# Second buffers for the activated rows of layer 2 in a two-layer graph network on one core

## The chip, the core and the metric

The kernel runs on one core of a Trainium2 chip. The core has a matrix engine (PE, with its weight loads PEld), a vector engine (DVE), an activation engine (ACT), a general engine (POOL) and a sync engine (SP) that here only issues transfers; 16 DMA engines move the data. The metric is the device time of one execution in microseconds (us), as the median of several runs.

## The reference, cut to what matters

```python
h = relu(layernorm(x)); x = x + attention_layer(h, src, dst)          # layer 1
h = relu(layernorm(x))                                                # layer 2
hW = h @ W_kernel + W_bias                  # (50000, 256)
h_self, h_all = split(hW, 2)
msg = h_all[src] + (edge_attr @ We_kernel + We_bias)
deg = in_degree[dst]
x = x + h_self + segment_sum(msg * clip(deg, 1), dst)
```

There are 50,000 nodes of 128 features and 50,000 edges, sorted by `dst`. Only layer 2 is touched by the change.

## The kernel before, in words

The kernel has three stages in a row: a table of keys and values (up to about 600 us of the profile), layer 1 (to about 1190 us) and layer 2 (from about 1200 us to the end). Each engine has its own program, written out by hand, and the programs are held together by counters (semaphores): `wait(engine, counter, value)` holds an engine until a counter has reached a value, `.then_inc(counter, 1)` raises it when an instruction is done.

Layer 2 works in 50 batches of 10 tiles; a tile is 100 nodes and the window of 128 edges that end in them. For batch k and tile t:

- SP loads the 100 x 10 node rows with their two layernorm numbers into `xn1` (`nodes1`, L692 to L695, four slots; the load of batch m waits until batch m-4 has been summed), ten windows of edge features into `eaw` (`features`, L685 to L690, four slots) and stores the result (`store1`, L697 to L701).
- POOL gathers, for each tile, the 128 rows of the edges' source nodes by an indirect transfer into `xs1` (`gathers1`, L820 to L827, four slots). Before each second gather t of batch k it waits until ACT has used tiles up to t+1 of batch k-4.
- ACT makes two activated tiles (`relu1`, L1697 to L1709): `hn1` from the node rows (L1704) and `hs1` from the gathered rows (L1707). Before each even tile it waits on `R.ha`, the counter of PE's pairs (L1703).
- DVE builds the one-hot edge-to-node matrix `member` (L1384) and moves PE's results out of the banks: `rows_out` (L1394), `features_out` (L1402), `turned_out` (L1410) and `sums` (L1420), which adds the node rows and gives the output.
- PE works in steps (`step1`, L2025 to L2045). Step k starts with `features_sum(k, 0)` (L1987), then come five `rows_sum` (L1991 to L2001), each of two tiles: it transposes `hn1` (L1998) and multiplies `hs1` by `member` (L1999) into one bank and raises `R.ha` by one. Between them stand the projections `project1` (L2010 to L2012) of this batch and the one before, and `turn_back` (L2021).

`hn1` and `hs1` have room for one batch (`hn1 = hn`, `hs1 = vw`, L233 and L234), so ACT may write tile t of batch k only when PE has read tile t of batch k-1. That makes ACT at most one batch ahead of PE, and POOL, which trails ACT by four slots, at most five.

Of PE's matmuls, one step has 78: 20 at L1987, 10 at L1998, 20 at L1999, 18 at L2010 to L2012 and 10 at L2021. The order of the work is fixed for each engine; only the waits decide when it runs. Layer 2's PE program is a loop over four steps for batches 2 to 45 (L2102 to L2105); ACT's, DVE's and POOL's are written out in full.

Two more tiles in on-chip memory have no user in layer 2: the part of `q` behind `oT` (columns 1200 on) and `prod`, both last used in layer 1. ACT starts layer 2 only after `long_done[0]` (L1753), when layer 1 is over.

Of the kernel before, what the change touches and what calls it, by code (L numbers as in the profile page):

```python
# [11 lines left out]
ACT = mybir.ActivationFunctionType  # L12
AX_X = mybir.AxisListType.X

N, D, E, HEADS, DE = 50000, 128, 50000, 4, 64
CH = D // HEADS
NODES = 100
TILES = N // NODES
WIN = 128
B = 10  # L20
# [44 lines left out]
def wait(eng, sem, value):  # L65

    if not isinstance(value, int) or value > 0:
        eng.wait_ge(sem, value)
# [66 lines left out]
def build(nc, x, edges, ea, Wq, bq, Wk, bk, Wv, bv, Ws, bs, W1, b1, We, be, out):  # L135
# [7 lines left out]
    with ExitStack() as ctx:  # L143
        def sb(name, shape, dt=F32):
            return ctx.enter_context(nc.sbuf_tensor("sb_" + name, shape, dt))

        def bank(name):
            return ctx.enter_context(nc.psum_tensor("ps_" + name, [128, 512], F32))
# [5 lines left out]
        ident = sb("ident", [128, 128])  # L154
# [19 lines left out]
        q_raw = sb("q", [128, 2 * B * D])  # L174
# [14 lines left out]
        vw = vw_raw[:].rearrange("e (t c) -> e t c", t=B)  # L189
        prod = prod_raw[:].rearrange("e (t c) -> e t c", t=B)  # L190
        hn = hn_raw[0:NODES, :].rearrange("n (t c) -> n t c", t=B)
# [37 lines left out]
        xs1 = kv_raw[:, 0:4 * B * XW].rearrange("e (s t c) -> e s t c", s=4, t=B)  # L229
        eaw = kv_raw[:, 4 * B * XW:4 * B * (XW + EW)].rearrange("e (s t c) -> e s t c", s=4, t=B)  # L230
        xn1 = xn_raw[0:NODES, 0:4 * B * XW].rearrange("n (s t c) -> n s t c", s=4, t=B)
        y1 = xo_raw[0:NODES, 0:4 * B * D].rearrange("n (s t c) -> n s t c", s=4, t=B)
        hn1 = hn  # L233
        hs1 = vw  # L234
        haT = hT_raw[:, 0:3 * 8 * NODES].rearrange("c (g h t n) -> c g h t n", g=3, h=2, t=4)
        aeT = mT_raw[0:EW + 1, 0:2 * B * NODES].rearrange("c (s t n) -> c s t n", s=2, t=B)
        oT = q_raw[:, 0:3 * 4 * NODES].rearrange("c (g t n) -> c g t n", g=3, t=4)
# [99 lines left out]
        banks = [bank(f"b{n}") for n in range(8)]  # L337
# [120 lines left out]
        P, A, R = Table(), Attend(), Message()  # L458
# [1125 lines left out]
        def _(act):  # L1584
# [112 lines left out]
            def relu1(k, t):  # L1697
                if t == 0:
                    act.wait_ge(R.xn[k % 4], 16 * (k // 4 + 1))
                if t % 5 == 0:  # L1700
                    act.wait_ge(R.xs[k % 4][t // 5], 16 * 5 * (k // 4 + 1))
                if t % 2 == 0:
                    wait(act, R.ha, 5 * (k - 1) + t // 2 + 1)  # L1703
                nc.scalar.activation(hn1[:, t, :], xn1[:, k % 4, t, 0:D], ACT.Relu,  # L1704
                                     scale=xn1[:, k % 4, t, D:D + 1], bias=xn1[:, k % 4, t, D + 1:XW]
                                     ).then_inc(R.relu, 1)
                nc.scalar.activation(hs1[:, t, :], xs1[:, k % 4, t, 0:D], ACT.Relu,  # L1707
                                     scale=xs1[:, k % 4, t, D:D + 1], bias=xs1[:, k % 4, t, D + 1:XW]
                                     ).then_inc(R.relu, 1)  # L1709

# [43 lines left out]
            for k in range(BATCHES):  # L1754
                for t in range(B):
                    relu1(k, t)
# [4 lines left out]
        def _(pe):  # L1761
# [229 lines left out]
            def rows_sum(s, j):  # L1991
                k = s.k
                n = 5 * k + j
                pe.wait_ge(R.relu, s.count(2 * B, 4 * j + 4))
                wait(pe, R.ha_sb, s.count(5, j - 1))
                for t in (2 * j, 2 * j + 1):
                    at = (t % 2) * NODES
                    nc.tensor.transpose(banks[n % 2][:, at:at + NODES], hn1[:, t, :], ident[0:NODES, 0:NODES])  # L1998
                    ins = nc.tensor.matmul(banks[n % 2][:, at + 2 * NODES:at + 3 * NODES], hs1[:, t, :],  # L1999
                                           member[:, (k + 3) % 4, t, :], start=True, stop=True)  # L2000
                ins.then_inc(R.ha, 1)  # L2001

# [128 lines left out]
```

## Time and profile before

| | us |
|---|---|
| three runs without a profile | 2101.73, 2109.67, 2113.67 |
| their median | 2109.67 |
| the profiled execution, device time | 2092.29 |
| its span, first to last instruction | 2090.5 |
| layer 2 in it | about 890 |

The profiled execution is 17.4 us below the median and 9.4 us below the lowest of the three runs. Spans and starts in a profile are microseconds from its first instruction. A row of the timeline has the start, the duration, the engine, the line, what is written and read, the count of merged instructions and, in brackets, how long the engine had been idle and what released it. "issue" and "remote" as a releaser mean that the profile found no instruction that had just ended.

### The profile page before, as it was taken

How to read it: one execution, taken by the hardware profiler on the slowest of the kernel's cores; microseconds unless marked ns; L12 is line 12 of the kernel's file. 1: busy time of each engine (PE TensorE's matmuls, PEld its weight loads, DVE VectorE, ACT ScalarE, POOL GpSimd, SP SyncE). 2: the span in 40 equal slices, each digit the busy share in tenths (PEclk: the TensorE clock that was granted, in tenths of full speed). 3: DMA queues.
4: the chain of work that ended last, by engine and by line, in shares of the span. 5: the costliest groups of instructions: out<-in, count | busy, mean ns of one | idle time of the engine just before them, and what ended most of it. 6: DMA issues, size and time to landing. Idle time of an engine off the chain costs nothing.

```text
span 2090.5 us, 34477 instructions
## 1 busy us (share of the span) xinstructions
PE 1562.4 (75%) x10545; PEld 1324.3 (63%) x10546; DVE 1347.9 (64%) x3688; ACT 1031.2 (49%) x2501; POOL 1092.3 (52%) x1202
## 2 busy tenths in 40 slices
PE   6888883777787778877778514777877887777787
PEld 4677663667777777776777513666665665555665
DVE  8877631777777787777778703555555555555565
ACT  6787872444444444445444123544444454444453
POOL 2544425556665666655665075555555555555530
PEclk9999996999999999999999856998998888999999
DMA  8898872445455554545454142555554454555442
GB/s 240 276 300 274 299 227 80 130 130 149 135 147 144 145 146 139 150 133 148 130 151 127 56 107 67 121 124 134 121 119 118 120 124 118 130 123 121 119 113 62
DMA packets 162552, 302.85 MB, mean 145 GB/s; under 512 B 104113, under 2 KB 107703, under 8 KB 157524
## 3 DMA queue, kind: packets, MB, share of 16 engines
q1 hardware_dynamic: 121503, 201.19, 33.0%
q0 software_dynamic: 40896, 99.90, 19.7%
q8 instruction: 62, 1.02, 0.2%
q14 instruction: 91, 0.75, 0.1%
HBM read 196.84 MB, written 104.12 MB: 144 GB/s over the span
## 4 chain that ended last, share of the span: by engine, by line
PE 41%; DVE 20%; issue 18%; another core or an unknown queue 14%; DMA 4%; ACT 1%; SPq 1%; POOL 1%; DVEq 0%; ACTq 0%; POOLq 0%
PE ps_b L1891 6%; PE ps_b L1999 5%; PE ps_b L1987 4%; PE ps_b L2010 3%; PE ps_b L1791 3%; PE ps_b L2011 3%; PE ps_b L2012 3%; DMA sb_kv<-in_x 3%; PE ps_b L2021 3%; DVE sb_member L1175 2%; PE ps_b L1924 2%; PE ps_b L1998 2%; PE ps_b L1879 2%; DVE sb_q L1410 2%
## 5 line engine op out<-in xcount | busy, mean ns | idle before, releaser
L797 POOL DMA_INDIRECT sb_kv<-kv_rows,sb_src_all x500 | 502.4, 1005 | 363.6 <-DVE sb_vw L1235 146.3
L825 POOL DMA_INDIRECT sb_kv<-x_rows,sb_src_all x500 | 473.4, 947 | 403.6 <-ACT sb_vw L1707 201.4
L1704 ACT ACTIVATE sb_hn<-sb_xn 100x128 f32<-100x128 f32 x500 | 242.1, 484 | 485.6 <-remote 195.4
L1394 DVE COPY sb_hT<-ps_b 128x400 f32<-128x400 f32 x250 | 142.1, 569 | 196.2 <-remote 79.7
L1707 ACT ACTIVATE sb_vw<-sb_kv 128x128 f32<-128x128 f32 x500 | 239.4, 479 | 0.0
L1632 ACT ACTIVATE sb_hn<-sb_xn,sb_nstat 100x128 f32<-100x128 f32 x500 | 231.2, 494 | 0.0
L1791 PE MATMUL ps_b<-sb_w,sb_memberT 128*125 128x256 f32 x800 | 199.0, 387 | 22.0 <-DVE sb_xn L915 12.1
L2021 PE MATMUL ps_b<-sb_ident,sb_q 128*100 128x128 f32 x500 | 93.0, 306 | 141.6 <-DVE sb_q L1410 100.7
L1924 PE MATMUL ps_b<-sb_vw,sb_member 128*100 128x128 f32 x1000 | 140.2, 292 | 70.0 <-DVE sb_vw L1235 70.0
L1999 PE MATMUL ps_b<-sb_member,sb_vw 128*128 128x100 f32 x1000 | 185.7, 291 | 0.0
L1654 ACT COPY sb_memberT<-ps_b 100x512 f32<-100x512 f32 x150 | 76.1, 508 | 208.9 <-PE ps_b L1879 123.7
L1924 PEld LDWEIGHTS ps_b<-sb_vw,sb_member 128*100 128x100 f32 x1000 | 123.7, 179 | 79.9 <-DVE sb_vw L1235 79.9
L1791 PEld LDWEIGHTS ps_b<-sb_w,sb_memberT 128*125 128x125 f32 x800 | 144.7, 191 | 44.8 <-issue 18.3
L1999 PEld LDWEIGHTS ps_b<-sb_member,sb_vw 128*128 128x128 f32 x1000 | 166.4, 209 | 9.8 <-issue 9.8
L1998 PE MATMUL ps_b<-sb_ident,sb_hn 100*128 100x100 f32 x500 | 133.1, 266 | 49.7 <-issue 39.8
L1187 DVE TENSOR_TENSOR sb_prod<-ps_b,sb_kv 128x512 f32<-128x512 f32 x150 | 89.3, 596 | 118.8 <-PE ps_b L1891 65.3
L2021 PEld LDWEIGHTS ps_b<-sb_ident,sb_q 128*100 128x100 f32 x500 | 58.8, 141 | 159.6 <-DVE sb_q L1410 93.5
L1987 PE MATMUL ps_b<-sb_member,sb_kv 128*65 128x100 f32 x1000 | 119.9, 274 | 49.0 <-issue 18.3
L1987 PEld LDWEIGHTS ps_b<-sb_member,sb_kv 128*65 128x65 f32 x1000 | 108.4, 156 | 74.2 <-issue 54.7
L1384 DVE TENSOR_SCALAR sb_member<-sb_iota,sb_drel_all,sb_wdeg_all 128x100 f32<-128x100 f32 x500 | 145.0, 339 | 0.1
L1646 ACT COPY sb_q<-ps_b 100x512 f32<-100x512 f32 x150 | 76.2, 508 | 133.0 <-remote 100.8
L1235 DVE TENSOR_TENSOR sb_vw<-sb_kv,ps_b 128x1280 f32<-128x1280 f32 x50 | 74.4, 1488 | 101.9 <-remote 97.4
(184 smaller groups left out, 3428.8 us busy)
## 6 DMA issues: line engine op xcount, KB each, us to landing
kv_rows<-sb_kv SPq DMA_DIRECT2D x26, 1120.0 KB
sb_xn<-x_rows SPq DMA_DIRECT2D x50, 507.8 KB
sb_xn<-in_x SPq DMA_DIRECT2D x50, 500.0 KB
out_rows<-sb_xo SPq DMA_DIRECT2D x49, 500.0 KB
x_rows<-sb_xo SPq DMA_DIRECT2D x24, 1015.6 KB
sb_kv<-in_edge_attr SPq DMA_DIRECT2D x500, 32.0 KB
sb_kv<-in_x SPq DMA_DIRECT2D x28, 560.0 KB
kv_rows<-sb_xn SPq DMA_DIRECT2D x13, 1120.0 KB
```

Of the source, the lines that this page charges most:

```text
L797: pool.indirect_dma_start(out=kvs[:, k % 4, t, :], out_offset=None, in_=kv_rows, in_offset=bass.IndirectOffsetOnAxis(ap=src_all[:, n:n + 1 ...
L825: pool.indirect_dma_start(out=xs1[:, k % 4, t, :], out_offset=None, in_=x1, in_offset=bass.IndirectOffsetOnAxis(ap=src_all[:, n:n + 1], ax ...
L1384: ins = dve.tensor_scalar(member[:, (k + 3) % 4, t, :], iota[:], drel_all[:, n:n + 1], wdeg_all[:, n:n + 1], ALU.is_equal, ALU.mult)
L1632: nc.scalar.activation(hn[:, t, :], xn[:, k % 5, t, :], ACT.Relu, scale=nstat[:, n, 0:1], bias=nstat[:, n, 1:2]).then_inc(A.relu, 1)
L1704: nc.scalar.activation(hn1[:, t, :], xn1[:, k % 4, t, 0:D], ACT.Relu, scale=xn1[:, k % 4, t, D:D + 1], bias=xn1[:, k % 4, t, D + 1:XW]).th ...
L1707: nc.scalar.activation(hs1[:, t, :], xs1[:, k % 4, t, 0:D], ACT.Relu, scale=xs1[:, k % 4, t, D:D + 1], bias=xs1[:, k % 4, t, D + 1:XW]).th ...
L1791: ins = nc.tensor.matmul(banks[2 + n % 4][0:ROWS, (t % 2) * 2 * D:(t % 2 + 1) * 2 * D], hpT[:, (3 * b + g) % 4, (t - first) * ROWS:(t - fi ...
L1924: ins = nc.tensor.matmul(ps[0:NODES, (t - first) * D:(t - first + 1) * D], member[:, k % 3, t, :], vw[:, t, :], start=False, stop=t == las ...
L1987: ins = nc.tensor.matmul(banks[2 + n % 2][0:EW, (t - 5 * i) * NODES:(t - 5 * i + 1) * NODES], eaw[:, k % 4, t, :], member[:, (k + 3) % 4, ...
L1998: nc.tensor.transpose(banks[n % 2][:, at:at + NODES], hn1[:, t, :], ident[0:NODES, 0:NODES])
L1999: ins = nc.tensor.matmul(banks[n % 2][:, at + 2 * NODES:at + 3 * NODES], hs1[:, t, :], member[:, (k + 3) % 4, t, :], start=True, stop=True)
L2021: ins = nc.tensor.transpose(banks[6 + (3 * k + g) % 2][0:NODES, t * D:(t + 1) * D], oT[:, g, t, :], ident[:])
```

## The change

The rows of layer 2 that ACT makes get a second buffer each, used by odd batches. The second `hn1` is 1280 columns of `q` behind `oT`, the second `hs1` is `prod`. ACT's wait on `R.ha` looks back two batches where it looked back one, so for batches 0 and 1 it is gone. PE reads the buffer of its batch.

```diff
-        hn1 = hn
-        hs1 = vw
+        hn1 = (hn, q_raw[0:NODES, 3 * 4 * NODES:3 * 4 * NODES + B * D].rearrange("n (t c) -> n t c", t=B))
+        hs1 = (vw, prod)
...
                 if t % 2 == 0:
-                    wait(act, R.ha, 5 * (k - 1) + t // 2 + 1)
-                nc.scalar.activation(hn1[:, t, :], xn1[:, k % 4, t, 0:D], ACT.Relu,
+                    wait(act, R.ha, 5 * (k - 2) + t // 2 + 1)
+                nc.scalar.activation(hn1[k % 2][:, t, :], xn1[:, k % 4, t, 0:D], ACT.Relu,
...
-                nc.scalar.activation(hs1[:, t, :], xs1[:, k % 4, t, 0:D], ACT.Relu,
+                nc.scalar.activation(hs1[k % 2][:, t, :], xs1[:, k % 4, t, 0:D], ACT.Relu,
...
-                    nc.tensor.transpose(banks[n % 2][:, at:at + NODES], hn1[:, t, :], ident[0:NODES, 0:NODES])
-                    ins = nc.tensor.matmul(banks[n % 2][:, at + 2 * NODES:at + 3 * NODES], hs1[:, t, :],
+                    nc.tensor.transpose(banks[n % 2][:, at:at + NODES], hn1[k % 2][:, t, :], ident[0:NODES, 0:NODES])
+                    ins = nc.tensor.matmul(banks[n % 2][:, at + 2 * NODES:at + 3 * NODES], hs1[k % 2][:, t, :],
                                            member[:, (k + 3) % 4, t, :], start=True, stop=True)
```

## Rows read from the trace of the kernel before

**Rows 1.** The page: span, then busy tenths of PE and POOL in 40 slices

```profile
span 2090.5 us, 34477 instructions
...
PE   6888883777787778877778514777877887777787
...
POOL 2544425556665666655665075555555555555530
```

**Rows 2.** Windows of layer 2: columns PE, PEld, DVE, ACT, POOL busy, PEclk, DMA share, GB/s

```profile
1299.30:2015.02 715.72, 557.23 (x3354) 443.11 (x3355) 399.20 (x989) 348.35 (x861) 406.88 (x430) 0.90 0.51 122
2029.69:2064.97 35.28, 33.70 (x235) 27.51 (x234) 27.73 (x69) 24.42 (x60) 0.00 (x0) 1.00 0.30 84
```

**Rows 3.** Waits from 1300 to 2000 us: total, times, longest

```profile
POOL sb_kv L825 <- ACT sb_vw L1707: 183.6, 78, 4.5
ACT sb_hn L1704 <- remote: 166.4, 42, 7.3
ACT sb_hn L1704 <- PE ps_b L1999: 158.3, 81, 4.9
```

**Rows 4.** PE's first use of ACT's rows, L1998, from 1300 to 2000 us

```profile
L1998 PE MATMUL ps_b<-sb_ident,sb_hn x422: 248/252/375, 1300.2 to 1997.9; 100*128 100x100 f32 x141
its engine sat idle before it (us, times) until:
  issue: 0.3, 2
  DVE sb_hT L1394: 0.2, 1
```

**Rows 5.** Timeline of one step in the middle of layer 2, 1503 to 1521 us

```profile
1503.51 0.94 POOL L825 DMA_INDIRECT sb_kv<-x_rows,sb_src_all  x1 [3.12 <-ACT sb_vw L1707]
...
1505.27 0.32 SPq L695 DMA_DIRECT2D sb_xn<-x_rows  x1
...
1509.01 0.64 PE L2021 MATMUL ps_b<-sb_ident,sb_q 128*100 128x128 f32 x4 [1.19 <-issue]
...
1515.37 0.94 POOL L825 DMA_INDIRECT sb_kv<-x_rows,sb_src_all  x1 [0.30 <-issue]
...
1517.87 0.69 DVE L1420 TENSOR_TENSOR sb_xo<-ps_b,sb_xn 100x512 f32<-100x512 f32 x1 [4.59 <-remote]
...
1518.22 0.49 ACT L1704 ACTIVATE sb_hn<-sb_xn 100x128 f32<-100x128 f32 x1 [4.37 <-remote]
...
1520.13 0.97 POOL L825 DMA_INDIRECT sb_kv<-x_rows,sb_src_all  x1 [3.83 <-ACT sb_vw L1707]
```

**Rows 6.** Timelines of the start of layer 2, 1200 to 1286 us

```profile
1200.75 0.74 SPq L695 DMA_DIRECT2D sb_xn<-x_rows  x2
...
1210.88 0.49 ACT L1704 ACTIVATE sb_hn<-sb_xn 100x128 f32<-100x128 f32 x1 [36.61 <-issue]
...
1223.75 0.48 ACT L1707 ACTIVATE sb_vw<-sb_kv 128x128 f32<-128x128 f32 x1
...
1243.38 0.68 DVE L1402 COPY sb_memberT<-ps_b 65x500 f32<-65x500 f32 x1 [26.09 <-issue]
...
1250.85 0.94 POOL L825 DMA_INDIRECT sb_kv<-x_rows,sb_src_all  x1 [0.30 <-issue]
...
1259.48 0.58 DVE L1394 COPY sb_hT<-ps_b 128x400 f32<-128x400 f32 x1 [14.95 <-issue]
...
1260.20 0.40 PE L1998 MATMUL ps_b<-sb_ident,sb_hn 100*128 100x100 f32 x1 [39.59 <-issue]
...
1263.34 0.94 POOL L825 DMA_INDIRECT sb_kv<-x_rows,sb_src_all  x1 [0.30 <-issue]
...
1269.58 0.94 POOL L825 DMA_INDIRECT sb_kv<-x_rows,sb_src_all  x1 [0.30 <-issue]
...
1279.14 0.57 DVE L1394 COPY sb_hT<-ps_b 128x400 f32<-128x400 f32 x1 [18.56 <-remote]
...
1281.05 0.94 POOL L825 DMA_INDIRECT sb_kv<-x_rows,sb_src_all  x1 [10.53 <-ACT sb_vw L1707]
...
1284.87 1.02 PE L1987 MATMUL ps_b<-sb_member,sb_kv 128*65 128x100 f32 x10
```

## The prediction

> **What bounds the kernel now.** I read the page first, then a table of windows, then the list of waits, and last the timelines. The page shows layer 2 as the last 17 slices, with PE at 7 to 8 tenths and POOL at 5 [rows 1]; the change touches nothing before them. The windows show what a step costs. A step has 78 matmuls, so the first window (x3354) holds 43 steps in 715.72 us, 16.64 us a step, and the second (x235) three steps in 35.28 us, 11.76 us a step [rows 2]. The work of a step is the same in both. What differs is that POOL issues no gather in the second; PE is then busy 96% of the time, in the first 78%. So in most of layer 2 a step loses 4.9 us to something that comes with the gathers.
>
> The timeline of one step shows where. PE's four transposes of L2021 start at 1509.01 and take 0.64 us, yet DVE's L1420, which needs them, starts at 1517.87 after 4.59 us of idleness [rows 5]. ACT's L1704, free since it had used up its one batch, starts at 1518.22, "remote". In between POOL issued ten gathers, the first at 1503.51, the last at 1515.37, and paused; the late events come 1.6 us after the last gather had ended (1515.37 + 0.94 = 1516.31). I read this as increments by PE that reach the other engines late while POOL gathers without a pause, and promptly once it pauses. The profile doesn't say why; the matmuls' ends are modelled, so it may be the matmuls themselves that end late.
>
> The start of layer 2 is the same thing at length. POOL's first 46 gathers need only what ACT does early, and it issues them in one burst, one each 1.25 us, the last at 1269.58 [rows 6]. In this burst PE issues nothing for 39.6 us up to 1260.20, and DVE gets single late counts at 1243.38, 1259.48 and 1279.14. The last comes 8.6 us after POOL stopped (1270.52), and with it everything runs again.
>
> Does anyone wait for ACT, which the change frees? PE's L1998, the first reader of ACT's rows, had 0.5 us of idleness ahead of it in 422 instructions, none of it put down to ACT [rows 4]. ACT waited 324.7 us in the same stretch, for PE [rows 3]; POOL waited 183.6 us for ACT. POOL's wait costs nothing in itself: its gathers are four batches ahead of ACT.
>
> **The change part by part.** *The removed waits.* Five waits of batch 1 go (batch 0 had none); the other 240 look one batch further back. The instructions stay 20 on ACT a batch. I cost the waits at nothing: a wait that is met at once is part of ACT's time, and ACT has 50% idle time in layer 2 to cover it (348.35 of 715.72 us busy [rows 2]). *The second buffers* lie in memory that layer 2 doesn't use; no transfer, no instruction, no wait is added for them. I cost them at nothing as well.
>
> *The middle of layer 2.* ACT has always used up its allowance. A second batch doesn't change its rate: pair j of batch k+2 is now released by the same count of `R.ha` that released pair j of batch k+1. So ACT, and POOL behind it, do the same work at the same moment of a step, for one batch later. PE's wait for ACT was nothing and stays nothing. Gain 0; cost 0 if the node rows come in time, which are now needed one step sooner. SP issued one such load at 1505.27 [rows 5]; it would have to be there when ACT starts its batch at 1518.22, 13.0 us later. No row gives the landing; the nearest bound is the start of layer 2, where loads issued from 1200.75 let ACT begin at 1210.88, so 10.1 us at most under heavy traffic [rows 6]. That leaves 2.9 us. If the cover is gone, ACT is late by some us at tile 0 with more than a batch in hand, and nobody waits for it. From below: no gain either, since no waiter exists. I take 0.
>
> *The start of layer 2.* Here the change acts. Before, ACT stops at tile 4 of batch 1 (last row before the stop at 1223.75), gets two more tiles at 1259.48, and POOL stops after the sixth gather of batch 5, because gather 6 waits for ACT's tile 7 of batch 1 [rows 6]. After, batch 1 needs no count. ACT does its last six tiles in about 5 us more (an estimate: 348.35 us for 861 instructions is 0.40 us each [rows 2], 12 of them 4.9 us), and batch 2 stops where batch 1 stopped. POOL then goes on for ten gathers more. These take 1263.34 - 1250.85 = 12.5 us. The burst ends at 1283.0 instead of 1270.5, and the release, now 1279.14, comes at about 1291.6. PE's second step starts that much later. From both sides: 0 if the release has its own clock and not POOL's pause; 19.7 us if PE's counts come through at intervals like the last one (1259.48 to 1279.14) and one interval more is needed. I take 12.5, since in both timelines the counts come shortly after the pause. If the 8.6 us of draining grow with the burst (46 gathers to 56), another 1.9 us are added; this goes to the range.
>
> *The end of layer 2.* POOL is now one batch further ahead, so its 500 gathers are over one step sooner, and one more step runs at 11.76 us instead of 16.64 us: -4.9 us [rows 2]. From both sides: 0, if the last gathers hinder nobody, and -9.8 us, if it is worth two steps.
>
> *The sum:* 0 + 12.5 - 4.9 = +7.6 us on the profiled execution: 2092.3 + 7.6 = 2099.9 us. The median of the runs shown lies 17.4 us above this execution, and I carry the difference unchanged: 2109.7 + 7.6 = **2117.3 us**, 0.36% slower. About 0.5% (10.5 us) is what a measurement of this kernel can tell from no change, so this is inside it.
>
> One rule speaks the other way. The rows show a regular gap of ACT in each step, 42 times 4.0 us, while PE has none before L1998 [rows 3, 4]; by them the second buffer is worth nothing in the middle. The Trainium skill (Perfetto Trace Analysis, Identifying Performance Opportunities) says that the same gap repeating on the engine that should be saturated can mean too few buffers for the next tile. Read for ACT, that rule would promise a gain. The engine that should be saturated is PE, and PE's repeated gap is before L2021, whose operands the change doesn't touch.
>
> **The rivals.** *A, nothing at all.* The late counts at the start have a cause of their own that ends at 1279 whatever POOL does, and the end gains nothing. For it: the profile names no releaser. Against: the late events follow POOL's pauses in both timelines. Time 2109.7 us.
>
> *B, slower.* The place is the start of layer 2, the mechanism the spacing of PE's late counts. They came at 1243.38, 1259.48 and 1279.14, 16.1 and 19.7 us apart [rows 6]. If the longer burst catches one more interval in place of 12.5 us, the start costs 19.7 us and the sum is 19.7 - 4.9 = +14.8 us: 2124.5 us. It decides once the count that frees PE misses POOL's pause at 1283. Against it: at 1279.14 the count came within 8.6 us of the pause.
>
> *C, faster.* POOL's pauses, 183.6 us in 42 steps, are ACT's waits handed on [rows 3]. If a batch in hand lets ACT, and with it POOL, run on where they now stop, the gathers spread evenly, and PE's counts may come through with less delay. Were a quarter of the pauses' time saved, it would be 46 us: 2064 us; the most is POOL's own rate, 12.5 us for a step of 16.64 us, over 43 steps 178 us. Against it: ACT is faster than PE and uses up any allowance, after which it stops at the same place. This is also the rule of the skill as a mechanism, and by that rule the trace agrees only in that the gap repeats.
>
> **How the numbers follow.** The forecast gets 0.45, A 0.17, B 0.18, C 0.20. Of the forecast's share a third (0.15) lies beyond +10.5 us: the longer draining gives +9.5, and a step is no more even than the waits in it, up to 7.3 us each [rows 3]. Slower by over 0.5%: 0.15 + 0.18 = 0.33. Within 0.5%: 0.30 + 0.17 = 0.47. Faster: 0.20. The range reaches up to B with the 4 us by which the highest run stands above the median, and some more: 2132. Down it takes in A, the 8 us by which the lowest run stands below the median, and the weak end of C: 2092. Outside are most of C and a little of B, about 0.2.
>
> **What would show it.** Right: in the changed kernel POOL's first pause comes after the sixth gather of batch 6, near 1283 us, PE's second step starts near 1297 instead of 1284.87 [rows 6], the steps in the middle stay at 16.6 us, PE before L1998 still never waits, ACT's total wait stays near 325 us in 1300 to 2000, and four steps run at 11.76 us at the end. Wrong: a step of clearly less or more than 16.6 us; a second step that starts no later than before; or PE waiting for ACT. The first would mean that the depth of ACT's buffer governs the gathers' rhythm, which I hold to be PE's.

## The result, and the profile after

The changed kernel took 2113.44 us (median of 20 runs, 2102.39 to 2124.96), the kernel before 2108.47 us (median of 20 runs, 2092.2 to 2113.84). The ratio of the two sets is put at 1.004, with a 95% interval of 1.0022 to 1.0058; the two medians by themselves are 5.0 us apart, 0.24%. So the change costs some 5 to 8 us, 0.2 to 0.4%. That is small, but it is there. The profiled execution took 2114.26 us.

The page of the changed kernel, as in [rows 1]:

```profile
span 2112.5 us, 34477 instructions
...
PE   6888874777788877777878314877878777778797
...
POOL 2544435655665566656653174555555555555520
```

PE's hole at the start of layer 2 is deeper (a 3 and a 1 where it had a 5 and a 1), and POOL is through a little earlier in the second to last slice (2 for 3). The windows of the changed kernel, cut as in [rows 2] (columns PE, PEld, DVE, ACT, POOL busy, PEclk, DMA share, GB/s). The first has 43 steps, the second four:

```profile
1316.27:2039.89 723.62, 567.12 (x3354) 450.92 (x3355) 401.09 (x990) 348.69 (x861) 401.08 (x422) 0.89 0.50 120
2039.89:2086.93 47.04, 44.93 (x313) 36.67 (x312) 36.99 (x92) 24.41 (x60) 0.00 (x0) 1.00 0.33 91
```

Four steps at the end run without gathers, at 47.04 / 4 = 11.76 us; before there were three. The 43 steps ahead of them took 16.83 us each, against 16.64.

The waits of the changed kernel from 1300 to 2000 us, as in [rows 3]. ACT's rows now have two names, since the second buffers lie in `q` and `prod`:

```profile
POOL sb_kv L825 <- ACT sb_prod L1707: 99.2, 39, 4.4
POOL sb_kv L825 <- ACT sb_vw L1707: 95.0, 44, 4.4
ACT sb_q L1704 <- PE ps_b L1999: 89.8, 41, 5.0
ACT sb_hn L1704 <- PE ps_b L1999: 78.1, 43, 4.7
ACT sb_q L1704 <- remote: 74.9, 19, 6.1
...
ACT sb_hn L1704 <- remote: 65.8, 17, 6.5
```

ACT waited 89.8 + 78.1 + 74.9 + 65.8 = 308.6 us in these four rows, 324.7 before. The rows of L1704 that are put down to "issue" are not shown, here or in [rows 3]; with them (58.2 us here, 32.2 before) it is 366.8 and 356.9 us. POOL waited 194.2 us for ACT, 183.6 before. The engine that got a second batch of room waits as much as it did. PE's first use of ACT's rows in the same stretch, as in [rows 4], has nothing under the heading of idle time:

```profile
L1998 PE MATMUL ps_b<-sb_ident,sb_q x210: 249/251/374, 1301.4 to 1987.3; 100*128 100x100 f32 x105
L1998 PE MATMUL ps_b<-sb_ident,sb_hn x204: 249/251/374, 1317.2 to 1997.9; 100*128 100x100 f32 x102
its engine sat idle before it (us, times) until:
who waited for it (us, times):
```

The start of layer 2 in the changed kernel, as in [rows 6]:

```profile
1201.72 1.90 PE L1987 MATMUL ps_b<-sb_member,sb_kv 128*65 128x100 f32 x10 [15.27 <-DMA sb_kv<-in_edge_attr]
...
1248.16 0.68 DVE L1402 COPY sb_memberT<-ps_b 65x500 f32<-65x500 f32 x1 [27.42 <-remote]
...
1264.96 0.57 DVE L1394 COPY sb_hT<-ps_b 128x400 f32<-128x400 f32 x1 [15.64 <-issue]
...
1265.68 0.40 PE L1998 MATMUL ps_b<-sb_ident,sb_hn 100*128 100x100 f32 x1 [41.98 <-issue]
...
1283.03 0.94 POOL L825 DMA_INDIRECT sb_kv<-x_rows,sb_src_all  x1 [0.30 <-issue]
1294.36 0.57 DVE L1394 COPY sb_hT<-ps_b 128x400 f32<-128x400 f32 x1 [28.34 <-remote]
...
1296.28 0.94 POOL L825 DMA_INDIRECT sb_kv<-x_rows,sb_src_all  x1 [12.31 <-ACT sb_vw L1707]
```

POOL's last gather of the burst starts at 1283.03 and ends at 1283.97; DVE gets the count it needs at 1294.36. The two late counts ahead of it, at 1248.16 and 1264.96, still fall inside the burst, after 27.42 and 15.64 us of DVE's idleness, much as in the kernel before (26.09 and 14.95 us [rows 6]). Only the third is later than it was: it comes after 28.34 us instead of 18.56. PE's second step starts at 1300.36, which is 98.64 us after the first (83.86 before).

The two spans differ by 22.0 us, far more than the two medians. PE's step starts (the first L1987 of each step) split it up:

| stretch | before | changed | difference |
|---|---|---|---|
| up to the first step of layer 2 | 1201.01 | 1201.72 | +0.7 |
| first to second step | 83.86 | 98.64 | +14.8 |
| second to eighth | 97.9 | 99.8 | +1.9 |
| eighth to 45th (37 steps) | 614.01 | 626.30 | +12.3 |
| 45th to 50th | 68.2 | 60.5 | -7.7 |
| behind it | 25.5 | 25.5 | 0 |

The start and the end are what the prediction spoke of. The 12.3 us in the middle are not, and need an explanation of their own: either the change does something there, or the two executions are an unequal pair. The first profile was 16 us below its kernel's median, the second is at its own.

### The profile page after: what moved, and what is told of

It is laid out like the page before. It is cut to its first block, busy times and chain, and to the rows that moved or that the text cites. A ratio compares the mean times of both kernels' runs of the same rounds, so it can differ in the third digit from the quotient of the medians.

```text
span 2112.5 us, 34477 instructions
## 1 busy us (share of the span) xinstructions
PE 1573.4 (74%) x10545; PEld 1330.5 (63%) x10546; DVE 1348.9 (64%) x3688; ACT 1033.8 (49%) x2501; POOL 1095.7 (52%) x1202
## 4 chain that ended last, share of the span: by engine, by line
PE 38%; DVE 21%; issue 18%; another core or an unknown queue 15%; DMA 4%; POOL 1%; ACT 1%; SPq 1%; DVEq 0%; POOLq 0%
PE ps_b L1891 6%; PE ps_b L1999 4%; PE ps_b L1987 4%; PE ps_b L2010 3%; PE ps_b L2012 3%; PE ps_b L2011 3%; DMA sb_kv<-in_x 3%; PE ps_b L2021 3%; PE ps_b L1791 3%; DVE sb_member L1175 2%; PE ps_b L1924 2%; DVE sb_member L1384 2%; PE ps_b L1998 2%; PE ps_b L1879 2%
## 5 line engine op out<-in xcount | busy, mean ns | idle before, releaser
L1704 ACT ACTIVATE sb_hn<-sb_xn 100x128 f32<-100x128 f32 x250 | 121.2, 485 | 268.2 <-remote 93.5
L1704 ACT ACTIVATE sb_q<-sb_xn 100x128 f32<-100x128 f32 x250 | 121.0, 484 | 217.3 <-PE ps_b L1999 99.9
L1791 PE MATMUL ps_b<-sb_w,sb_memberT 128*125 128x256 f32 x800 | 200.0, 388 | 20.8 <-DVE sb_xn L915 12.1
L2021 PE MATMUL ps_b<-sb_ident,sb_q 128*100 128x128 f32 x500 | 94.1, 309 | 134.5 <-DVE sb_q L1410 81.7
L1987 PE MATMUL ps_b<-sb_member,sb_kv 128*65 128x100 f32 x1000 | 122.2, 276 | 64.5 <-issue 25.8
L1987 PEld LDWEIGHTS ps_b<-sb_member,sb_kv 128*65 128x65 f32 x1000 | 109.2, 158 | 91.9 <-issue 68.5
L2021 PEld LDWEIGHTS ps_b<-sb_ident,sb_q 128*100 128x100 f32 x500 | 59.9, 142 | 151.2 <-DVE sb_q L1410 76.7
L1916 PE MATMUL ps_b<-sb_w,sb_hT 128*100 128x128 f32 x1000 | 138.2, 279 | 0.0
L1870 PE MATMUL ps_b<-sb_w,sb_hT 128*100 128x128 f32 x1000 | 137.2, 277 | 0.0
L2010 PE MATMUL ps_b<-sb_hT,sb_w 128*128 128x400 f32 (+1 forms) x300 | 127.0, 509 | 8.2 <-issue 5.3
```

Of the source, the lines that this page charges most:

```text
L1704: nc.scalar.activation(hn1[k % 2][:, t, :], xn1[:, k % 4, t, 0:D], ACT.Relu, scale=xn1[:, k % 4, t, D:D + 1], bias=xn1[:, k % 4, t, D + 1: ...
L1791: ins = nc.tensor.matmul(banks[2 + n % 4][0:ROWS, (t % 2) * 2 * D:(t % 2 + 1) * 2 * D], hpT[:, (3 * b + g) % 4, (t - first) * ROWS:(t - fi ...
L1916: nc.tensor.matmul(ps[0:NODES, (t - first) * D:(t - first + 1) * D], hnT[:, k % 3, t, :], w0[:, 3, :], start=False, stop=False)
L1987: ins = nc.tensor.matmul(banks[2 + n % 2][0:EW, (t - 5 * i) * NODES:(t - 5 * i + 1) * NODES], eaw[:, k % 4, t, :], member[:, (k + 3) % 4, ...
L2010: nc.tensor.matmul(to, w1[:, 0:D], haT[:, g, 0, 0:last - first, :], start=True, stop=False)
L2021: ins = nc.tensor.transpose(banks[6 + (3 * k + g) % 2][0:NODES, t * D:(t + 1) * D], oT[:, g, t, :], ident[:])
```

## The experiments

The theory: all that the change does is to let POOL issue ten more gathers in a row, which keeps PE's counts from the other engines for the time of ten gathers, and to take ten gathers out of the end. Its rivals are that the memory places cost something, that ACT's depth itself does, that PE's late counts have their own time, and that the middle got slower.

Each ratio is to the kernel before on the same chip; that kernel took 2105.25 us on the chip of the first four experiments, and on that of the others 2075.64 and, in a second set, 2074.7 us. The list of waits and the timelines of each kernel give its burst and its steps, as above.

**The buffers alone.**

```diff
-                    wait(act, R.ha, 5 * (k - 2) + t // 2 + 1)
+                    wait(act, R.ha, 5 * (k - 1) + t // 2 + 1)
```

> The changed kernel with ACT's wait one batch back again: only the places of the second buffers are left of the change. Theory (all that the change does comes from the wait): equal to the kernel before in everything, time within 0.3% of it, second step of PE about 84 us after the first (98.6 us in the changed kernel), middle steps 16.6 us. Rival (the new places in memory cost something in each step, since the changed kernel's middle steps were 16.9 us and not 16.6): middle steps stay at 16.9 us and the time is about 13 us above the kernel before.

Measured: 2109.11 us, ratio 1.0015 (0.9996 to 1.0033), second step 83.3 us after the first, three steps at 11.76 us at the end. With the wait undone the start and the end are those of the kernel before, so they come from the wait. The middle had 16.77 us a step in this profile, between the two, and left that question open. The 0.15% above the kernel before, within its interval, can be looked at more closely, since each run has the mean granted clock of PE on record. Seven of the 12 runs here and seven of the 23 of the kernel before had a clock below 0.90 and took 2112.6 and 2111.6 us in the mean; the others had 0.904 to 0.920 and took 2102.6 and 2103.3 us. Compared kind with kind there is next to no difference; what differs is how many runs were of each kind.

**ACT keeps its second batch, POOL's lead goes down by one.**

```diff
-                        wait(pool, R.relu, 2 * B * (k - 4) + 2 * (t + 2))
+                        wait(pool, R.relu, 2 * B * (k - 3) + 2 * (t + 2))
```

> The changed kernel with POOL three batches ahead of ACT instead of four, so that ACT keeps its second batch and POOL's opening burst is as long as before (56 gathers instead of 66). Theory (the loss at the start is the length of the burst): second step of PE about 84 us after the first, three steps at 11.8 us at the end instead of four, time within 0.3% of the kernel before. Rival (ACT's second batch itself delays PE at the start, or in the middle): 98 us, or middle steps of 16.9 us; the time stays at that of the changed kernel or above it, as the gain at the end is gone too (ratio 1.004 to 1.008).

Measured: 2109.78 us, ratio 1.0014 (0.9993 to 1.0035), second step after 84.9 us, POOL's first pause after 56 gathers as before, three steps at 11.76 us at the end, 16.84 us a step in the middle. The rival's 98 us did not come; its 16.9 us in the middle nearly did, and that is taken up with the last pair of runs. ACT's second batch is there and costs nothing at the start once POOL's burst has its old length. This is the change's effect taken back at the other end of the chain.

**The kernel before, POOL's lead two batches instead of four.**

```diff
-                        wait(pool, R.relu, 2 * B * (k - 4) + 2 * (t + 2))
+                        wait(pool, R.relu, 2 * B * (k - 2) + 2 * (t + 2))
```

> The kernel before with POOL two batches ahead of ACT instead of four: its opening burst has 36 gathers instead of 56. Theory (12.5 us at the start for ten gathers, 4.9 us back at the end): second step of PE about 59 us after the first (83.9 before), one step at 11.8 us at the end instead of three, middle steps 16.6 us, time -25.0 + 9.8 = -15.2 us, ratio 0.993. Rival (PE's late counts have a time of their own): 84 us at the start and only the loss at the end, +9.8 us, ratio 1.005.

Measured: 2094.97 us, ratio 0.9944 (0.9926 to 0.9963). Its timeline at the start:

```profile
1242.63 0.94 POOL L825 DMA_INDIRECT sb_kv<-x_rows,sb_src_all  x1 [0.30 <-issue]
...
1248.70 0.67 DVE L1402 COPY sb_memberT<-ps_b 65x500 f32<-65x500 f32 x1 [26.83 <-remote]
1251.40 0.94 POOL L825 DMA_INDIRECT sb_kv<-x_rows,sb_src_all  x1 [7.82 <-ACT sb_vw L1707]
...
1256.13 1.02 PE L1987 MATMUL ps_b<-sb_member,sb_kv 128*65 128x100 f32 x10
```

POOL stops after 34 gathers (the expectation said 36), and the first late count (DVE's L1402) comes at 1248.70, 5.1 us after the last gather's end. That by itself shows nothing: it comes after 26.83 us of idleness, and in the kernel before the same count came after 26.09 us, at 1243.38, in the midst of the burst [rows 6]. What shows something is what follows. There it took two more late counts, 14.95 and 18.56 us of idleness apart, before PE went on; here PE goes on at once, 29 us earlier. So the moment at which PE is set free follows POOL, while the first late count, in a burst that is long enough, comes some 26 to 27 us on whether POOL pauses or not. The second step came after 54.8 us, 29.0 us earlier for 22 gathers less, 1.3 us each.

The saving of 29 us did not all arrive: the time fell by 10 to 12 us. The steps in the middle took 17.1 us here and not 16.6. A window from the eighth to the 45th step of this kernel shows it:

```profile
1358.38:1992.41 634.03, 511.04 (x2888) 392.19 (x2887) 345.00 (x851) 300.93 (x740) 349.51 (x372) 0.80 0.50 119
```

The work is the same (2888 matmuls), but PE's granted clock was 0.80 where it was 0.90 before. 33 of these 37 steps lay between 16.9 and 17.2 us, while in the kernel before they go up and down between 13 and 22 us. Its six runs were within 2.6 us of each other (2093.73 to 2096.34). The layer has, it seems, an even rhythm at a lower clock and an uneven one at a higher, and which of them a kernel falls into is worth 0.5 us a step. In the even one the clock changes in time with the step. Four stretches out of two steps of this kernel, which start at 1497.42 and 1514.50:

```profile
1498.30:1508.30 10.00, 8.07 (x63) 6.93 (x60) 5.59 (x14) 4.95 (x12) 5.46 (x6) 0.99 0.41 93
1508.80:1515.20 6.40, 5.58 (x16) 3.50 (x17) 3.35 (x9) 2.90 (x8) 3.77 (x4) 0.52 0.68 166
1515.40:1525.40 10.00, 8.04 (x62) 6.91 (x60) 5.58 (x14) 4.95 (x12) 5.49 (x6) 0.99 0.40 87
1525.80:1532.20 6.40, 5.48 (x15) 3.39 (x16) 3.34 (x9) 3.00 (x8) 3.76 (x4) 0.52 0.62 163
```

Each step runs some 10 us at the full clock (2.4 GHz) and nearly 7 us at half of it (1.2 GHz). The clock falls while PE is idle, in the 3.25 us ahead of its L2021 at 1509.62; L2021 and the projections behind it then run at half clock. Whether the step keeps time with the clock or the clock with the step, no run tells.

**The kernel before, with pauses in POOL's opening burst.**

```diff
+                    if t % 5 == 0 and 0 < B * k + t < 60:
+                        m = k if t == 5 else k - 1
+                        pool.wait_ge(R.xs[m % 4][t // 5 - 1 if t == 5 else 1], 16 * 5 * (m // 4 + 1))
```

> The kernel before, but in its first six batches POOL waits before each fifth gather until the five before have landed: eleven pauses in the opening burst, of perhaps 2 to 3 us each. Theory (PE's increments get through when POOL pauses, and are held up only while it runs on): the stall at the start goes nearly away; PE's second step comes 20 to 30 us after its first instead of 83.9, the time falls by 40 to 60 us, ratio 0.971 to 0.981. Rival (what counts is how many gathers have been issued or are under way, not whether they come without a pause): the stall ends as before after the 56th gather, with the pauses added to it: 84 us plus 11 times 2.5 us, about 110 us, ratio about 1.012.

Measured: 2124.2 us, ratio 1.0076 (1.0054 to 1.0099), slower. The pauses did what the theory said: the second step came after 28.9 us, the next at 13.8, 20.2, 20.1 and 19.3 us. But the seventh step came 79.8 us after the sixth. The timeline of that place (lines are shifted by three against the kernel before, so L2001 is its L1998, L2024 its L2021):

```profile
1309.38 0.94 POOL L828 DMA_INDIRECT sb_kv<-x_rows,sb_src_all  x1 [4.97 <-DMA sb_kv<-x_rows,sb_src_all]
...
1361.58 0.43 PE L2001 MATMUL ps_b<-sb_ident,sb_hn 100*128 100x100 f32 x1 [39.89 <-issue]
...
1382.45 1.09 PE L2024 MATMUL ps_b<-sb_ident,sb_q 128*100 128x128 f32 x4 [19.42 <-DVE sb_q L1413]
1383.25 0.94 POOL L828 DMA_INDIRECT sb_kv<-x_rows,sb_src_all  x1 [10.55 <-ACT sb_vw L1710]
```

After its last pause, at 1309.38, POOL runs on without stopping to 1383.25 - 10.55 = 1372.70 us, 51 gathers in a row. It makes good there the lead of four batches that it had been kept from, PE having gone ahead in the meantime. PE pays with 39.89 and 19.42 us of idleness, nearly the same two figures as at the start of the kernel before (39.59 and 18.6 us). (The rival's ratio of 1.012 came nearer, but its mechanism, a first stall of 84 us with the pauses on top, did not happen either.) So my gain of 40 to 60 us was wrong: pauses put the stall off, they don't do away with it, because the lead has still to be built. What costs is the length of a burst, wherever it is.

**The extra ten gathers put into the middle.**

```diff
-                    wait(act, R.ha, 5 * (k - 2) + t // 2 + 1)
+                    wait(act, R.ha, 5 * (k - (2 if k >= 20 else 1)) + t // 2 + 1)
```

> The changed kernel, but ACT looks back one batch up to batch 19 and two from batch 20 on, so that the ten extra gathers come in the middle of layer 2 and not in the opening burst. Theory (ten gathers in a row more cost 12.5 to 15 us wherever they come): second step of PE at 84 us as in the kernel before, then around batch 20 one or two steps that are together 10 to 15 us longer than their neighbours, and four steps at 11.8 us at the end; time as the changed kernel, ratio about 1.004. Rival (only the opening burst is harmful): no long step around batch 20, and with the gain at the end a time of 4.9 to 7.7 us below the kernel before, ratio 0.997.

Measured: 2087.74 us, ratio 1.0056 (1.0041 to 1.007). The start is that of the kernel before (84.6 us). Step 20, counted from 0 as in the edit, started 33.9 us after step 19, with neighbours of 15.0 and 12.1 us; four steps at the end ran at 11.76 us. The timeline around it:

```profile
1565.03 0.94 POOL L825 DMA_INDIRECT sb_kv<-x_rows,sb_src_all  x1 [1.52 <-ACT sb_prod L1707]
...
1586.24 0.95 POOL L825 DMA_INDIRECT sb_kv<-x_rows,sb_src_all  x1 [0.30 <-issue]
1589.42 0.67 PE L2021 MATMUL ps_b<-sb_ident,sb_q 128*100 128x128 f32 x2 [16.54 <-DVE sb_q L1410]
...
1592.44 0.94 POOL L825 DMA_INDIRECT sb_kv<-x_rows,sb_src_all  x1 [5.25 <-ACT sb_prod L1707]
```

POOL ran from 1565.03 to 1587.19 without a pause, 18 gathers in a row. PE, which had last issued at 1571.85, got its next operands 2.2 us after the end. From the start of step 18 to that of step 21 it was 61.0 us, where three steps at 16.6 take 49.8, so the ten extra gathers cost 11 us here. That is the change's loss reproduced some 380 us behind the start of the layer, with the early part left as it was, and the start is not special. (The ratio is a little above the 1.003 that the changed kernel has on this chip, see below; nothing here explains the rest.)

**Rows or gathers?** Two kernels that leave part of the layer's data out. The first gathers 64 rows of each window instead of 128:

```diff
-                    pool.indirect_dma_start(out=xs1[:, k % 4, t, :], out_offset=None, in_=x1,
-                                            in_offset=bass.IndirectOffsetOnAxis(ap=src_all[:, n:n + 1], axis=0)
+                    pool.indirect_dma_start(out=xs1[0:64, k % 4, t, :], out_offset=None, in_=x1,
+                                            in_offset=bass.IndirectOffsetOnAxis(ap=src_all[0:64, n:n + 1], axis=0)
```

> The kernel before with gathers of 64 rows instead of 128 in layer 2 (the other 64 rows of each window are left as they were, so the sums are of other data); as many gathers, at the same places. Theory A (what holds PE's counts up is the writing or moving of the gathers' many row descriptors or rows): stall at the start about halved, 40 to 55 us, and middle steps of 12 to 14 us; time 2105 - 30 - 43 x 3.5 = about 1925 us. Theory B (it is the gather instruction as such, one after another): 84 us and 16.6 us a step stay, time within 0.5% of the kernel before, unless POOL needs less time for one.

Measured: 2100.89 us, ratio 1.0119 (1.0094 to 1.0145). The second step came 83.6 us after the first: half the rows, the same stall. The middle took 17.1 us a step, in the even rhythm again:

```profile
1371.09:2004.63 633.54, 510.55 (x2887) 393.19 (x2888) 343.21 (x852) 301.49 (x742) 335.25 (x372) 0.82 0.42 100
```

DMA share and bytes are down (0.42 and 100 GB/s from 0.51 and 122 [rows 2]), POOL's time for a gather hardly (335.25 / 372 = 901 ns; 406.88 / 430 = 946 before [rows 2]). Fewer rows to move bought nothing; the 1.2% above the kernel before (25 us) are for the most part the even rhythm, 0.5 us in each of the 37 steps. By itself this doesn't separate the number of gathers from the time that POOL spends on them.

The second leaves every other gather out:

```diff
                     if t % 2 == 0:
                         wait(pool, R.relu, 2 * B * (k - 4) + 2 * (t + 2))
+                    else:
+                        continue
...
-                    act.wait_ge(R.xs[k % 4][t // 5], 16 * 5 * (k // 4 + 1))
+                    act.wait_ge(R.xs[k % 4][t // 5], 16 * (3, 2)[t // 5] * (k // 4 + 1))
```

> The kernel before with every second gather of layer 2 left out (odd tiles use the rows that lie there, so the sums are of other data): 250 gathers of 128 rows instead of 500. Theory (the time goes with the number of gathers issued, as halving their rows left all as it was): the opening burst has 28 gathers, second step of PE 40 to 48 us after the first (83.9); a step in the middle costs 11.8 us plus half of 4.9 us, 14.2 us; time 38 us + 44 x 2.4 us = about 145 us less than before, ratio 0.93. Rival (a step costs 16.6 us for another reason, such as the loads of the edge features): 16 us or more in the middle, and 35 to 45 us less in all, ratio 0.98.

Measured: 1820.41 us, ratio 0.8771 (0.8751 to 0.8792). The start was as expected: 27 gathers in a row (28 expected), second step after 44.1 us. The steps behind it were all 11.76 us, every one of the 48, where I had expected 14.2. A long window of this kernel, and from its waits between 1300 and 1700 us POOL's longest and the only row of PE's matmuls:

```profile
1231.87:1760.00 528.13, 504.43 (x3508) 412.02 (x3507) 415.37 (x1035) 365.37 (x899) 211.48 (x220) 1.00 0.58 143
```

```profile
POOL sb_kv L827 <- ACT sb_vw L1709: 225.8, 160, 3.1
...
PE ps_b L2023 <- DVE sb_q L1412: 18.4, 35, 0.5
```

POOL gathers five tiles in each step and pauses several times, 160 times in 400 us, and PE is busy 96% of the time at full clock. So the 4.9 us that a step loses aren't a price per gather: at five a step nothing is lost, at ten all of it. Ten gathers take POOL 12.5 us, so 0.7 us of the 4.9 would be POOL's own rate if it never paused. Of the rest a part is the clock: the same 78 matmuls kept PE busy for 11.2 us of a step here, at a granted clock of 1.00, and for 13.0 us in the kernel before, at 0.90 [rows 2]. That what is left goes with gathers in an unbroken row fits the start, but this run doesn't show it for the middle, because it changed two things at once: there are half as many gathers, and they no longer come in rows (from the eighth step to the 45th mostly singly or in pairs, where the kernel before has rows of two to ten). It does show that the other loads don't slow a step by themselves, since the edge features' transfers were all still there (DMA share 0.58).

**Less lead still.** POOL one batch ahead of ACT, in the kernel before:

```diff
-                        wait(pool, R.relu, 2 * B * (k - 4) + 2 * (t + 2))
+                        wait(pool, R.relu, 2 * B * (k - 1) + 2 * (t + 2))
```

> The kernel before with POOL one batch ahead of ACT instead of four: its opening burst has 26 gathers (56 before, 36 with two batches). Theory: the start falls by the 14.5 us for ten gathers that the run with two batches showed (83.9 - 54.8 = 29.0 for twenty), so PE's second step comes 38 to 43 us after the first; the last steps lose one more 4.9 us; steps in between 17.1 us as there, since ACT's tiles still follow from PE and the gathers are still early enough. Time 2095.0 - 14.5 + 4.9 = 2085.4 us, ratio 0.990 to the kernel before. Rival (one batch of lead is too little, ACT waits for gathered rows): middle steps of 18 us or more, time above the kernel before.

Measured: 2046.21 us, ratio 0.9854 (0.9833 to 0.9874). That is 29 us below the kernel before, and below the changed kernel too: the best of the kernels that gather all their rows. POOL paused first after 22 gathers, not 26, and the second step came after 41.4 us; the middle stayed in the uneven rhythm:

```profile
1329.15:1934.50 605.35, 474.56 (x2887) 377.93 (x2886) 341.01 (x851) 299.59 (x741) 349.41 (x369) 0.91 0.51 124
```

16.36 us a step at a clock of 0.91. No step at the end ran at 11.76 us; that gain is gone. The last five steps took 85.7 us, against 66.8 in the second profile of the kernel before on this chip, so 19 us were lost there, against 43 us gained at the start (84.0 to 41.4). The expected 0.990 was too cautious since it took the 17.1 us of the run with two batches for the middle.

With the landing pauses of above in the first three batches besides:

```diff
+                    if t % 5 == 0 and 0 < B * k + t < 30:
+                        m = k if t == 5 else k - 1
+                        pool.wait_ge(R.xs[m % 4][t // 5 - 1 if t == 5 else 1], 16 * 5 * (m // 4 + 1))
```

> POOL one batch ahead of ACT, and in its first three batches a wait before each fifth gather until the five before have landed. There is no lead of four batches to be made good afterwards, which cost the kernel with pauses alone a second stall of 79.8 us. Theory (only gathers issued in a row hold PE up): second step of PE 25 to 32 us after the first, no step over 25 us behind it, middle steps 17.1 us; time that of the run with one batch of lead less 10 us, about 2075 us, ratio 0.986. Rival (a debt of PE's counts builds up that has to be paid once): the sum of the first six steps is as in the run with one batch of lead and without pauses, and so is the time.

Measured: 2058.02 us, ratio 0.9916 (0.9898 to 0.9933), worse than without them. The second step came after 30.9 us, but the fourth 37.6 us after the third, when POOL issued 19 gathers in a row to catch up. The first six steps took 131.6 us together, against 121.3 without pauses. It is the second stall of the kernel with pauses alone once more, in small, which I had thought gone with the long lead. The theory's form of this expectation fell, and the rival's too, as the sum was not equal but worse.

And POOL six tiles ahead, the least possible:

```diff
-                        wait(pool, R.relu, 2 * B * (k - 4) + 2 * (t + 2))
+                        wait(pool, R.relu, 2 * B * k + 2 * (t + 2 - 6))
```

> The kernel before with POOL six tiles ahead of ACT, the least that its ten-tile batches allow (40 tiles before, 10 in the run with one batch of lead): 22 gathers in the opening burst. Theory: four gathers of 1.4 us less at the start than there (second step of PE at 35 to 37 us), 2 us given back at the end, ratio 0.983 against 0.9854 of that run. Rival (the gathers now come too late for ACT and PE waits for ACT): steps of 17 us and more in the middle, ratio 0.99 or above.

Measured: 2186.64 us, ratio 1.055 (1.0514 to 1.0586). POOL's first pause came after six gathers and not after 22. The second step came after 32.1 us, the earliest but for the two kernels with pauses, but the steps in the middle took 19.6 us. The waits of this kernel, 1300 to 2000 us:

```profile
POOL sb_kv L825 <- ACT sb_vw L1707: 275.3, 72, 6.0
...
PE ps_b L1998 <- ACT sb_vw L1707: 176.8, 70, 5.0
...
ACT sb_hn L1704 <- DMA sb_kv<-x_rows,sb_src_all: 154.5, 36, 5.4
```

Here is what a lead that is too short looks like: ACT waits for gathered rows and PE waits for ACT ahead of L1998, 176.8 us in 70 waits. In the kernel before that row was 0.5 us and not for ACT [rows 4]. The least lead that doesn't starve PE is more than six tiles and at most ten.

**Both kernels a second time**, with no edit.

> The kernel before as it is, for a second profile and for the spread between two sets of its runs. Its first profile was of one of its fastest executions, with 16.59 us a step from the eighth step to the 45th. Theory (the changed kernel's 16.93 us a step there are mostly the choice of the execution): this profile shows 16.6 to 17.0, ratio 1.000 within 0.2%. Rival (the change makes each step in the middle longer): again 16.6 here, and 16.9 in the second profile of the changed kernel.

> The changed kernel as it is, a second profile. Theory: second step of PE at 98 us again, end with four steps at 11.8 us, middle within 0.15 us of the kernel before in the same call, ratio 1.003 to 1.006 (14.8 - 7.7 = 7 us of 2110). Rival: middle 0.3 us or more above the kernel before, and a ratio of 1.007 or more.

Measured: the kernel before 2073.81 us, ratio to itself 0.9993 (0.9977 to 1.0008); the changed kernel 2081.76 us, ratio 1.003 (1.0018 to 1.0042), second step after 95.6 us (84.0 in its pair), four steps at 11.76 us at the end (three). The windows from the eighth to the 45th step, of the kernel before in its first and in its second profile:

```profile
1382.75:1996.76 614.01, 478.46 (x2888) 381.74 (x2886) 342.75 (x850) 298.83 (x740) 348.88 (x369) 0.90 0.51 122
```

```profile
1368.89:1981.42 612.53, 484.33 (x2888) 385.36 (x2887) 343.63 (x852) 299.97 (x740) 351.00 (x370) 0.89 0.50 122
```

and of the changed kernel in its first and second:

```profile
1400.14:2026.44 626.30, 487.58 (x2887) 387.41 (x2886) 344.49 (x850) 299.40 (x740) 350.89 (x370) 0.89 0.50 120
```

```profile
1386.63:1994.58 607.95, 478.61 (x2887) 383.76 (x2888) 342.23 (x851) 299.88 (x742) 348.87 (x368) 0.90 0.51 123
```

37 steps took 614.0 and 612.5 us in the one, 626.3 and 608.0 us in the other. The changed kernel differs from itself by 18 us; its second middle is the shortest of the four. The kernel before came out at 16.55 us a step, as the rival had it, but the changed kernel at 16.43 and not at 16.9, so the rival fell. The second pair ran where the kernel before is 34 us faster, so each pair is compared within itself. Nor does it take another chip to get such scatter: the 20 runs of the changed kernel in the first set lie up to 22.6 us apart, the ten with a granted clock of 0.913 or more at 2102 to 2114 us, the seven below 0.90 at 2118 to 2125. So nothing in the middle can be put down to the change. A small effect could still hide in the scatter: with ACT one batch ahead the 37 steps took 614.0, 612.5 and 620.6 us (the buffers alone), with two batches 626.3, 608.0 and 623.3 us (POOL's lead one less), in the mean 3.5 us more, 0.1 us a step, where each group by itself spreads over 8 to 18 us.

The second pair split up as the first was:

| stretch | before | changed | difference |
|---|---|---|---|
| up to the first step of layer 2 | 1184.53 | 1190.98 | +6.5 |
| first to second step | 84.0 | 95.6 | +11.7 |
| second to eighth | 100.4 | 100.0 | -0.4 |
| eighth to 45th (37 steps) | 612.5 | 608.0 | -4.6 |
| 45th to 50th | 66.8 | 65.8 | -1.0 |
| behind it | 25.5 | 25.5 | 0 |

The 6.5 us of the first row stand ahead of anything that the change touches, and are scatter as well.

## Why the prediction was right

The forecast was 2117.3 us and +0.36%; measured were 2113.44 us and +0.40%, in the second set +0.30%. Of the kernel before these are 8.4 and 6.2 us (5.0 and 7.1 us by the medians alone), against the +7.6 us of the sum. That the total came so near is in part luck: it lies within the scatter, and the two terms that make it up were each off by some us in one pair or the other.

- **The waits and buffers, 0.** With the wait undone the start and the end went back to those of the kernel before, so neither comes from the places in memory. As a time the 0 is shown only within the interval's 0.33%, which is as much as the whole change; runs of the same clock were within 1 us of each other.
- **The middle, 0.** Right in its mechanism (PE never waited for ACT, ACT used up its allowance and waited on) and, by the second pair of profiles, in size as far as can be told, which is to some 0.1 to 0.3 us a step. The first pair seemed to speak against it. That the node rows come in time was not looked at by itself; it would have shown as a wait of PE.
- **The start, +12.5 us.** The place was right to the gather: the first pause is after the sixth gather of batch 6, at 1283.0. The size was 14.8 us in the first pair and 11.7 in the second. In the first pair the release came 10.4 us after the burst's end instead of 8.6, so there the longer draining of which I spoke took place; in the second it came after 8.3 us in both kernels, and the term was the mere length of ten gathers. One number in the text is a miscount: POOL's burst had 56 gathers and not 46, and has 66 and not 56 now. The difference of ten, on which the term rests, is not touched.
- **The end, -4.9 us.** One more step at 11.76 us, in both pairs. The last five steps together were 7.7 us shorter in the first pair; in the second 1.0 us, as the last steps with gathers happened to be long or short. More profiles tell the size better. In four with three such steps (the kernel before twice, the buffers alone, POOL's lead one less) the last five took 67.7 us in the mean, in three with four such steps (the changed kernel twice, the wait from batch 20 on) 63.1 us, which is 4.6 us less.
- **"Late while POOL gathers without a pause".** This reading of two timelines was the part that most needed a test. Five kernels bear it out: 34 gathers, 54.8 us to the second step; 56, 84 us; 66, 96 to 99 us; and the burst moved to step 20 or to the seventh step moves the stall with it. It holds for the moment at which PE is set free. The first late counts inside a long burst do come at much the same times whatever POOL does afterwards.
- **Rival A** (nothing at all) fell with the ratio's interval. **Rival B** (the counts' own spacing) priced the start at 19.7 us, too much; the last interval was 1294.36 - 1264.96 = 29.4 us and not 19.7. A spacing there is for the first counts, which came at 1243.38 and 1259.48 before and at 1248.16 and 1264.96 now, 16.1 and 16.8 us apart; but the burst took in no further one, and the last count followed the pause. **Rival C** (more depth evens out the gathers' rhythm) did not happen: POOL's pauses for ACT grew from 183.6 to 194.2 us. With it falls the reading, for ACT, of the Trainium skill (Perfetto Trace Analysis, Identifying Performance Opportunities) by which a repeated gap can mean too few buffers. The rule speaks of the engine that should be saturated, and the kernel with six tiles of lead agrees with it: there the repeated gap is PE's, 70 times ahead of L1998, and too few tiles are in hand.

## What to carry to other kernels

Before giving an engine a deeper buffer, look for someone who waits for that engine; here there was nobody, and the depth was only passed on upstream, where it lengthened the burst with which a producer starts. A lead has a price of its own when its building disturbs others: here ten tiles were enough, six starved PE, and forty cost 29 us against ten. And one profiled execution can be off by more than a small change is worth (18 us in the middle between two of the same kernel here), so a term must be looked for in its own place, and a second pair of profiles bounds what is left.

## What the runs showed of the hardware that I had not expected

- A gather of 64 rows holds PE's counts up as long as one of 128 (83.6 and 83.9 us for 56 of them), and takes POOL 901 ns instead of 946.
- Five gathers a step, with pauses between them, cost PE nothing (11.76 us a step, as with none), ten cost 4.9 us. Whether it is the number or the rows that matters in the middle was not told apart.
- PE's two waits in a burst of 51 to 56 gathers have much the same length in both places where there was one: 39.59 and 18.6 us at the start of the layer, 39.89 and 19.42 us in the seventh step. With 66 gathers the second grew, to 28.3 us as DVE's row has it. What holds up PE's counts is not shown: in every timeline PE's matmuls end by the model long before DVE starts, and no run told late increments from late matmuls.
- The burst slows SP as well, and where it waits for nobody. Its ten issues of one batch of edge features (L690), in the kernel before:

```profile
1204.06 5.61 SPq L690 DMA_DIRECT2D sb_kv<-in_edge_attr  x10
...
1211.54 28.30 SPq L690 DMA_DIRECT2D sb_kv<-in_edge_attr  x10
...
1246.13 32.92 SPq L690 DMA_DIRECT2D sb_kv<-in_edge_attr  x10
```

  There is no wait between the ten, and in the trace even its register moves, else some 0.03 us, mostly take 0.70 us there. With 64 rows a gather the last two rows are 29.61 and 31.87 us. So the burst does not hold up PE's counts alone. Whether the two have one cause is not shown, and it was not tested.
- The same program can run in an even rhythm of 17.1 us a step, at a granted clock of 0.80 to 0.82, or in an uneven one of 16.4 to 16.9 us at 0.89 to 0.91. These are mixtures of the clock's two levels, 1.2 and 2.4 GHz. One execution can go from one to the other: the kernel with pauses and a lead of four batches had 0.90 from 1480 to 1740 us, in steps of 13 to 20 us, and 0.80 from 1760 to 2000, where every step took 17.0 to 17.3 us. In the profiles the rhythm changed with POOL's lead (two batches even, one and four uneven) and with the rows of a gather, and none of my reasons foresaw it. It hid a good part of the gain of the kernel with two batches.
